# Inverse head lengths of a local-attention block: GpSimd power in place of a VectorE and ScalarE chain

## The chip, the cores and the metric

One core of a Trainium2 chip runs the whole program in one launch. The metric is device microseconds of one execution. The kernel before took 1195.36 us (median of three runs, 1194.01 to 1196.31).

## The reference

The input `x` holds 8 batches of 512 tokens by 128 features, fp32. A modulation vector made from `silu(c) @ wmod` gives each batch its shifts, scales and gates.

1. The first block ("a"): layer norm and modulation, projections to q, k, v, a 16-head attention of an unusual form (k against v, softmax, then q), gated and added to `x`. It needs 512x512 probabilities for every head and batch.
2. The second block ("b"): layer norm and modulation, then two layers (`L = 2`) of a small transformer, gated and added to `x`. Each layer does this:

```
h   = shift_token(x);  q, k, v = split(h @ wqkv)        # 8 heads of 64
q   = q / clip(norm(q), 1e-12) * qs;  k = k / clip(norm(k), 1e-12) * ksc
q, k = rotary_xpos(q, k)
o   = local_attention(q, k, v)                          # windows of 64, looking one window back
x   = x + o @ wo
h   = layernorm(shift_token(x));  x = x + (a * gelu(g)) @ w2 + b2
```

The change is about the one division `1 / clip(norm(.), 1e-12)`: for each token and head, the inverse square root of the sum of 64 squares. The scales `qs`, `ksc` are already folded into the rotary tables.

## The kernel before, in words

Block a is one stream of work called `a`: 8 batches, each 32 steps of scores on TensorE (L465), a negated row maximum on VectorE (L1191), `Exp` with row sums on ScalarE (L905), a reciprocal on VectorE (L1195), a small multiplication on GpSimd (L803) and the weighted sum on TensorE (L474).

Block b is three streams, `x`, `y`, `z` (s = 0, 1, 2), which work on the batches [0, 1, 2, 5], [3, 6] and [4, 7] in turn. Each batch passes through two layers, so there are 16 layer passes in all. Stream x starts while `a` still runs; y and z start when `a` is over. One layer pass has these parts:

- Projection of k and v, then q, one tile of 128 tokens at a time (TensorE, L523).
- Eight rotations, k's four tiles first (w = 1), then q's four (w = 0). For each: ScalarE squares the projection (L970), VectorE multiplies it by the cosine table (L1258) and, with halves swapped, by the sine table (L1262), and adds up the squares of each head (L1266, into `ss`); GpSimd adds the two products (L825, `b_rotary`). L1262 releases GpSimd's addition, L1266 comes right behind it on VectorE.
- Twice per layer pass (for k after its fourth rotation, for q after its fourth), the inverse lengths of four tiles and eight heads together, a 128x32 tile: VectorE clamps `ss` and multiplies by 2^20 (L1272, `b_norm`, which reads two SBUF tensors), ScalarE takes `Ln` (L978) and `Exp` with scale -0.5 (L980), and VectorE does a Newton step of three instructions (L1148, L1149, L1150, called from `b_rnorm`). All four VectorE instructions have two SBUF inputs. That makes 32 such chains in the program.
- GpSimd multiplies each tile by its inverse lengths (L833, `b_scale`), TensorE transposes it (L530), ScalarE copies it out (L984, L989).
- Local attention in eight units: scores (L541, L548), maximum (L1284), `Exp` in four pieces (L998), reciprocal (L1289), multiplication of the probabilities by it on GpSimd (L838), transposes (L558), weighted values (L569).
- Output projection (L579), layer norm, which has a Newton step of its own on 128x4 tiles by the same lines L1148 to L1150, hidden layer (L598), GELU (L1017), second projection (L604).

Every engine carries out its instructions strictly in the order written. That order is a string per engine (`ORDER`), which says for each next yield of work which stream it belongs to; `BANKS` says which of the eight PSUM banks each TensorE result gets. Both were laid down ahead of time. Semaphores hold each instruction until its inputs are there.

Of the kernel before, what the change touches and what calls it, by code (L numbers as in the profile page):

```python
# [65 lines left out]
B_CHAIN = LN_CHAIN + (2 * 2 + LN_CHAIN) * L  # L66
# [9 lines left out]
        "xaaaaaaaaaxxxaaxaaaaxxaaaxxaaaxxxaxxaxxxaxxxxxyxyyyyyyyxyyxxxxxxyxyyxxxxxxxxxxyyyyxxxxxxyyyyxyxxxyxx"
        "yyyxxyxxxxxyxyxxyyxxxyyxxyyyxyyxxxxxxyxxyxyyyyyyxzyzzzzzzzzzzxxxxxxzzxxzzzzxxyyyyyyyyzzzzyzxxxxxxyzz"
        "zzzzzzxxxzzxzyyzzzxzxzxxxzxyxyyxxyzxxzzxzzzzxyzxxyzxzzxzzxzzzzzyyxyxxxxxxzzxzzzzyyxxxxxyxzzxyyyzxzxx"
        "zyyyyxxzzyyxyxxxyzzzyzzzyzzzxyxxxzzzxzxzyxxxzyyyyyyzxxyzzyzxxxzxzzyzyyzxxyxxyyyyxyzxzzzxzzyyzzzzxzxx"
        "xxxxyyxyyxyyzzzzzzxxxxzxzxzzxzyzyyyxxzyxzxyzzzyyzzxxzzyzyyxzzxzxyyzyyxzyyxyzyxxyxyzxzzzyxxzzzxzxyxxy"  # L80
# [17 lines left out]
    "ACT": (
        "aaaaaaaaaaaaaaaaaaaaaaaaaaaaaaaaaaaaaaaaaaaaaaaaaaxaaaaaaxaaaaaaaaaaaaaaaaaaxaaxaaaxxxaxxxxaaxaxxaaa"
        "axxaaaxxxaaaaaxxaaaaxxxxaaaaaaaaaaaaaaaaaaaaaaaaaaaaaaaaaaaaaaaaaaaaaxxaxaxxaaaxaaaaaaaaaaaaaaaaaaxx"  # L100
        "xaxxaaxxaaxaaxaxaaaaaaxaaaaxaxaaaaxaaxaaaaxaaaxxaxxxxxxaxaxaaaaxxaaxxxaaaaxxaaaxxaxxaaaaxxaxaxxxxxax"
        "xxaxaxxaxaxaaaaxaxaxaaxaaaaaaaaaaaaxaaaxaxaaxxaxxxaxxxaaxaxaxaaaaxaaxaxxxaaxxaaaaxaxaxxaaaxxxxxxaaaa"
        "xxxxxxxxxxyyxyyxyyyyyxyyyxyyyxyxxxxxxxxxyxxyyxxxyxyxyxxyyyxxyxxyyxxxyyxxxyyxxxxxyxyxxyyxxyyyxyyxxyxy"
        "yyxzxxzzyzzzzzzzzzzxzxxxzzxxzxzzxyyxzzyyxxzzzzyyxyxzzxxxyyyzzzzxxyzzzzxxzzxzzxyyzzxxxxzxxxzxyxxyyzxx"
        "yyxzxyzxxyzzzxzzzxzzzyyxzzxzzyzxzzyyzxxxxyyxyxzzxzyzyxzxyxxyzzyxxyyyzxyxxzzyzxxzzzzzyzxzzxxxzzyxxxyz"
        "xxxxzyzxxzxyxxyyxyyxyxxzyyyyyzzzxzzzzxyyyzzzxxzzyyzyyyzzzxzzxxzzxxxzyxzyxzzxyzyyyzxxzzxzyzyyxxyyyzzz"
        "zzxzxzzyyzyzyxxxyyxxyyzxyyxxzxzyxxzyxxxxzyxxxxxzzzzzzzzyxxxzxxyzzyxzzzyzxzyyyyxyyzzyxyzzzyzxzyyyzyzx"
        "yxxzzzxyyxzxxzxyxyzyzxyxzzxyyxxxxyyyyxzzyyyyzxxxxxyzyxxyyxxxyxzxyxxxzxyxzxxyzyxxyxxxx"
    ),
    "POOL": (  # L110
        "aaaaaaaaaaaaaaaaaaaaaaaaaaaaaaaaaaaaaaxaxaxaxxxaxxaxxxaaxaaaxxaxxaaaaaaaaaaaaaaaaaaaaaaaaaxxaxaaaaaa"
        "aaaaaaxxxaxaxaaaaaaaaaaaaaaxxaaxxaxaaxxxxxxaxaaxxxxaaaaaxxxxaxxxaxaaaaaaaaaaaaaaaaxaxxaxaxaxxaxxaxax"
        "xaxxaxxaaaxaxxaxaxxxaxyyyyyyyyyyyxxxxxxxxxxxyyxyyyxxxxyyyxxxyxxxyxyxyyzzzzzzzzzzxxzzxxzzzzxxxxxxyyzx"
        "yyzxzyzxxxzxzyyzzyyyyxxxxxxyxyyyyxzzzzzzzzzzzyzyyzzxxzxzxyyxxzxyyxxxyxzzxzxxxxzzzzxxxxxxxxyyyyzzyyzz"
        "yyyyzzzzzzzzyyzzzzxyyyyxzxzxxzyyzxxyzxzxxzxzyyyxyxxyxxxxxxxxzzzzxxzzzzzyzzzyyzzyzzyyyyyyzyzyzxxzyyyx"
        "xyxzzxxxxxyyzxxyyxxxxyzyyxxyxxxxxx"
    ),
# [5 lines left out]
    "0123424024024023502350135023550224602640240240240240254024602450424602402402402402024062450140264623"  # L123
    "0340364013456022042002406234052042042042042052045204520402460240240240240240246204135024502450235024"
    "5024605240520154250235024602450246024660314603601630562402340621346260302402464016205135135602642042"
    "0642605450243503256052604010351300412140134013502350240240624601206504135123530530522301562042046230"
    "4513502466024604065060776776012023271207320170107675707675051270207007070723462146021206246036204723"
    "5072012701001701701010170170207606765606751050626743402713534036227271050512403050712705140712701315"
    "7053701256013760710362516702760717017060501273762516025676506743024067132076376023720510376341374027"
    "3062601206234175717031430214760416706570657405670650716560570176570656174707672572514750571232527660"  # L130
    "7060201707276407457123056736320156512305625407256076070176176707650214764757437015601615101637013017"
    "2370107127070360102502467310413206027607046152056135420565450135371013576560360414601763406430670471"
    "076516323521320734237401072107607076076076077"
# [1330 lines left out]
```

## Time and profile before

| what | value |
|---|---|
| median of three runs | 1195.36 us |
| the profiled execution | 1196.15 us |
| its span in the profile | 1194.3 us |
| granted TensorE clock, mean | 0.948 |
| TensorE matmul busy | 997.0 us (83%) |
| VectorE busy | 949.4 us (79%) |
| ScalarE busy | 918.2 us (77%) |
| GpSimd busy | 508.1 us (43%) |

Some 1.9 us of the profiled execution lie outside the span. A busy TensorE is not TensorE at its peak, since the ends of its matmuls are modelled. The profile's engines are PE (TensorE matmul), PEld (its weight load), DVE (VectorE), ACT (ScalarE), POOL (GpSimd), SP (SyncE). "Busy" leaves out waits. The last step of block a (L792 of batch 7) starts at 560.6 us; from there on only the streams of block b run.

### The profile page before, as it was taken

The page shows a single profiled execution, that of the slowest core. Times are in us where ns is not written, and L with a number is a line of the kernel's source. Part 1 is how long each engine was busy: PE and PEld are TensorE (multiplying, and loading weights), DVE is VectorE, ACT ScalarE, POOL GpSimd, SP SyncE. Part 2 cuts the span into 40 slices and gives each one's busy share as a digit, 9 for nine tenths or more (in the row PEclk, how much of TensorE's full clock was granted, in tenths as well). Part 3 has the DMA queues.
Part 4 walks back from the last instruction along what each step waited for, and adds up shares of the span by engine and source line. Part 5 has one row for each costly group of instructions (what it writes and reads, how often), then busy time and mean ns, then how long its engine had stood idle before and what let it go on. Part 6 is the DMA issues. An engine that isn't in the chain of part 4 may idle for free. (4 is left out here: it accounts for less than half of the span.)

```text
span 1194.3 us, 23996 instructions
## 1 busy us (share of the span) xinstructions
PE 997.0 (83%) x8124; PEld 510.0 (43%) x8124; DVE 949.4 (79%) x1947; ACT 918.2 (77%) x2782; POOL 508.1 (43%) x578
## 2 busy tenths in 40 slices
PE   2677787768888798778868897899999789999898
PEld 2232232223323352234336444655664357545664
DVE  4789898888869777986884699779769976789865
ACT  1698979899978988887659566868886587958983
POOL 5012143212105321343474058647823676348830
PEclk8699989999989898998989998999999999999999
DMA  5541305232204103001011001101110020001200
GB/s 206 180 142 36 106 1 146 62 107 71 72 0 130 43 28 115 10 10 24 1 31 34 10 1 32 33 1 32 33 41 10 10 63 16 18 1 32 46 20 27
DMA packets 28009, 59.18 MB, mean 50 GB/s; under 512 B 6192, under 2 KB 6384, under 8 KB 26736
## 3 DMA queue, kind: packets, MB, share of 16 engines
q1 hardware_dynamic: 27120, 56.33, 16.7%
q8 instruction: 67, 1.10, 0.4%
q10 hardware_dynamic: 768, 1.31, 0.3%
q14 instruction: 54, 0.44, 0.1%
HBM read 23.98 MB, written 18.87 MB: 36 GB/s over the span
## 5 line engine op out<-in xcount | busy, mean ns | idle before, releaser
L905 ACT ACTIVATE E<-psum,neg_max 128x512 f32<-128x512 f32 x512 | 346.6, 716 | 64.2 <-DVE neg_max L1191 45.9
L1191 DVE TENSOR_REDUCE neg_max<-psum 128x2 f32<-128x1024 f32 x256 | 307.5, 1214 | 58.7 <-PE psum L465 56.7
L465 PE MATMUL psum<-v_rows,k_rows 64*128 64x512 f32 x512 | 130.3, 514 | 106.0 <-ACT E L905 79.6
L998 ACT ACTIVATE rot_work<-psum,neg 128x128 f32<-128x128 f32 x512 | 184.3, 412 | 17.9 <-DVE neg L1284 11.0
L838 POOL TENSOR_TENSOR rot_work<-rot_work,rz 128x512 f32<-128x512 f32 x128 | 133.0, 1047 | 141.0 <-DVE rz L1289 140.9
L825 POOL TENSOR_TENSOR work<-work,rot_work 128x512 f32<-128x512 f32 x96 | 121.7, 1273 | 129.6 <-DVE rot_work L1262 129.3
L465 PEld LDWEIGHTS psum<-v_rows,k_rows 64*128 64x128 f32 x512 | 52.8, 196 | 250.6 <-ACT E L905 116.1
L803 POOL TENSOR_TENSOR qz<-qT,rz 128x32 f32<-128x32 f32 x128 | 30.8, 241 | 300.7 <-DVE rz L1195 299.8
L523 PE MATMUL psum<-wqkv_sb,hs 128*128 128x512 f32 x288 | 144.0, 622 | 6.8 <-DVE hs L1248 3.8
L474 PE MATMUL psum<-E,qz 128*32 128x512 f32 x1024 | 148.2, 653 | 0.2 <-POOL qz L803 0.2
L998 ACT ACTIVATION_READ_ACCUMULATOR rot_work<-psum,neg 128x1 f32 x512 | 126.7, 252 | 0.0
L905 ACT ACTIVATION_READ_ACCUMULATOR E<-psum,neg_max 128x1 f32 x512 | 119.8, 234 | 0.0
L1284 DVE TENSOR_REDUCE neg<-psum 128x4 f32<-128x512 f32 x128 | 85.5, 677 | 36.2 <-PE psum L548 36.1
L833 POOL TENSOR_TENSOR work<-work,rn 128x512 f32<-128x512 f32 x96 | 99.6, 1056 | 16.6 <-DVE rn L1150 16.6
L970 ACT ACTIVATE rot_work<-psum 128x512 f32<-128x512 f32 x128 | 77.9, 612 | 31.0 <-PE psum L523 22.3
L598 PE MATMUL psum<-work,w_sb 128*128 128x512 f32 (+1 forms) x192 | 94.0, 623 | 2.7 <-ACT work L1013 2.1
L558 PE MATMUL psum<-ident,rot_work 128*128 128x128 f32 x512 | 80.8, 286 | 15.5 <-POOL rot_work L838 8.8
L1008 ACT ACTIVATE prT<-psum 128x512 f32<-128x512 f32 x128 | 79.2, 636 | 11.5 <-PE psum L569 8.2
L1262 DVE TENSOR_TENSOR rot_work<-psum,rot 128x512 f32<-128x512 f32 x128 | 87.0, 679 | 0.0
L1266 DVE TENSOR_REDUCE ss<-rot_work 128x8 f32<-128x512 f32 x128 | 86.4, 675 | 0.0
L558 PEld LDWEIGHTS psum<-ident,rot_work 128*128 128x128 f32 x512 | 57.1, 143 | 45.6 <-POOL rot_work L838 26.3
L1258 DVE TENSOR_TENSOR work<-psum,rot 128x512 f32<-128x512 f32 x96 | 65.4, 681 | 12.6 <-ACT rot_work L970 12.3
(140 smaller groups left out, 1784.7 us busy)
## 6 DMA issues: line engine op xcount, KB each, us to landing
k_rows<-k_scr SPq DMA_DIRECT2D x128, 64.0 KB, 1.9
work<-v_al SPq DMA_DIRECT2D x16, 512.0 KB, 4.4
v_rows<-v_scr SPq DMA_DIRECT2D x124, 64.0 KB, 1.9
...
```

The source lines that it names most:

```text
L465: pe.matmul(bank, k_rows[r:r + 64, half, hh, P * j:P * (j + 1)], v_rows[r:r + 64, b % 2, hh, :], start=True, stop=True).then_inc(full, 1)
L474: last = pe.matmul(O_BANK[32 * q:32 * q + 32, :], qz[:, hh, j % QZ_SLOTS, q, :], E[:, (b * NG + g) % E_RING, q, :], start=(g == 0), stop=( ...
L523: pe.matmul(bank, hs[s][:, P * i:P * (i + 1)], wqkv_sb[:, l, INNER * c:INNER * (c + 1)], start=True, stop=True).then_inc(full, 1)
L558: last = pe.transpose(bank[:, P * w:P * (w + 1)], pr[s][:, u % PR_SLOTS, w, :], ident[:])
L598: pe.matmul(bank[0:CH[c]], w1_sb[:, l, o:o + CH[c]], h2T[s], start=True, stop=True).then_inc(full, 1)
L825: pool.tensor_tensor(qk_of(s, i, w), qk_of(s, i, w), sinp[s][:, n % 2, :], ALU.add).then_inc(rot_sum[s], 1)
L833: pool.tensor_tensor(v, v, rn[s][:, i, w, :].unsqueeze(2).broadcast_to([P, H, DH]), ALU.mult).then_inc((q_ready, k_ready)[w][s], 1)
L838: pool.tensor_tensor(pr[s][:, u % PR_SLOTS], pr[s][:, u % PR_SLOTS], rz2[s][:, u, :].unsqueeze(2).broadcast_to([P, 4, 2 * W]), ALU.mult).t ...
L905: act.activation(E[:, (b * NG + g) % E_RING, 2 * half + m, :], pair[:, m], ACT.Exp, bias=neg_max[:, n, m:m + 1], accum_out=z[:, n, m:m + 1 ...
L998: last = act.activation(pr[s][:, u % PR_SLOTS, w, :], bank[:, 2 * W * w:2 * W * (w + 1)], ACT.Exp, bias=neg2[s][:, u, w:w + 1], accum_out= ...
L1191: dve.tensor_reduce(neg_max[:, n, :], pair, AX.X, ALU.max, negate=True).then_inc(max_ready, 1)
L1262: dve.tensor_tensor(sinp[s][:, n % 2, :].rearrange("p (h a r) -> p h a r", h=H, a=2), bank.rearrange("p (h a r) -> p h a r", h=H, a=2)[:, ...
```

## The change

The chain of six instructions becomes two on GpSimd: a clamp and multiplication by 2^20 (`tensor_scalar`, one SBUF input, into `nt`), and `nt` to the power of a tile that holds -0.5 (`tensor_tensor` with `ALU.pow`, into `rn`). There is no Newton step. GpSimd waits for the sums (`ss_ready`) itself, then waits for its own first instruction. The tile `clamp` (2^20 everywhere, set up by a GpSimd memset at L781) becomes `minus_half`; `nlog` and two sets of semaphores go. The chain on VectorE and the two activations go from their streams, and GpSimd's stream gets them: for k after its fourth rotation, for q after its eighth. `ORDER` and `BANKS` are new on all engines; every other instruction stays as it is.

```diff
-B_CHAIN = LN_CHAIN + (2 * 2 + LN_CHAIN) * L
+B_CHAIN = LN_CHAIN + LN_CHAIN * L
 ORDER = {
...
-            pool.memset(clamp[:], SHIFT2).then_inc(s_clamp, 1)
+            pool.memset(minus_half[:], -0.5).then_inc(s_minus_half, 1)
...
+            def b_norm(s, k, l, w):            # pool
+                n = (k * L + l) * 2 + 2 - w
+                passed(pool, ss_ready[s], (k * L + l) * 2 * J + J * (2 - w))
+                pool.tensor_scalar(nt[s][:, :, w, :], ss[s][:, :, w, :], NORM_MIN2, SHIFT2, ALU.max, ALU.mult).then_inc(ss_all[s], 1)
+                pool.wait_ge(ss_all[s], n)
+                pool.tensor_tensor(rn[s][:, :, w, :], nt[s][:, :, w, :], minus_half[:], ALU.pow).then_inc(rn_ready[s], 1)
...
+                            if n == J - 1:
+                                b_norm(s, k, l, 1)
+                                yield
                             for i in {J: (0,), J + 1: range(1, J)}.get(n, ()):
                                 b_scale(s, k, l, i, 1)
                                 yield
+                        b_norm(s, k, l, 0)
+                        yield
                         for i in range(J):
                             b_scale(s, k, l, i, 0)
                             yield
...
-            def b_norm(s, k, l, w):            # act
-                act.wait_ge(ss_all[s], (k * L + l) * 2 + 2 - w)
-                act.activation(nlog[s][:, :, w, :], ss[s][:, :, w, :], ACT.Ln).then_inc(ss_log[s], 1)
-                act.wait_ge(ss_log[s], (k * L + l) * 2 + 2 - w)
-                act.activation(rn[s][:, :, w, :], nlog[s][:, :, w, :], ACT.Exp, scale=-0.5).then_inc(ss_rsqrt[s], 1)
...
-            def b_norm(s, k, l, w):            # dve
-                passed(dve, ss_ready[s], (k * L + l) * 2 * J + J * (2 - w))
-                v = ss[s][:, :, w, :]
-                dve.scalar_tensor_tensor(v, v, NORM_MIN2, clamp[:], ALU.max, ALU.mult).then_inc(ss_all[s], 1)
-
-            def b_rnorm(s, k, l, w):
-                dve.wait_ge(ss_rsqrt[s], (k * L + l) * 2 + 2 - w)
-                newton(ss[s][:, :, w, :], rn[s][:, :, w, :], nt[s][:, :, w, :], b_link_of(s, k)).then_inc(rn_ready[s], 1)
```

## Rows read from the trace of the kernel before

**Rows 1.** The page: busy us (share of the span) and instructions of each engine.
```profile
PE 997.0 (83%) x8124; PEld 510.0 (43%) x8124; DVE 949.4 (79%) x1947; ACT 918.2 (77%) x2782; POOL 508.1 (43%) x578
```
**Rows 2.** Busy time by stretch: us, each engine's busy (instructions), clock, DMA share.
```profile
0.00:562.00 562.00, 429.34 (x2861) 176.01 (x2862) 453.13 (x802) 461.93 (x1375) 163.05 (x266) 0.91 0.27 79
562.00:1194.00 632.00, 567.66 (x5271) 334.01 (x5266) 496.30 (x1146) 456.27 (x1407) 345.02 (x313) 0.98 0.10 23
```
**Rows 3.** The same view, PE PEld DVE ACT POOL, of eleven 20 us stretches.
```profile
600.00:620.00 20.00, 11.40 (x52) 6.50 (x51) 18.21 (x31) 9.43 (x22) 16.78 (x16) 0.89 0.00 0
...
700.00:720.00 20.00, 19.79 (x58) 8.60 (x58) 19.83 (x37) 12.67 (x26) 15.52 (x14) 1.00 0.00 1
...
940.00:960.00 20.00, 12.33 (x45) 6.47 (x46) 19.23 (x45) 8.43 (x17) 13.33 (x12) 0.75 0.04 14
...
1100.00:1120.00 20.00, 18.07 (x236) 12.11 (x234) 19.37 (x38) 17.32 (x67) 18.82 (x18) 1.00 0.21 48
sum 220.00, PE 196.18 PEld 99.97 DVE 211.75 ACT 151.34 POOL 156.15; mean PE 17.83 PEld 9.09 DVE 19.25 ACT 13.76 POOL 14.20
```
**Rows 4.** VectorE and ScalarE by line, from 562 us: xcount, busy us, mean ns, idle before.
```profile
L1272 DVE SCALAR_TENSOR_TENSOR ss<-ss,clamp 128x32 f32<-128x32 f32 x26 | 17.2, 666 | 0.3
L1149 DVE TENSOR_TENSOR nt<-nt,rn 128x32 f32<-128x32 f32 x26 | 14.1, 543 | 0.9
L1148 DVE SCALAR_TENSOR_TENSOR nt<-ss,rn 128x32 f32<-128x32 f32 x26 | 12.3, 472 | 2.9 <-ACT rn L980 2.8
L1150 DVE SCALAR_TENSOR_TENSOR rn<-nt,rn 128x32 f32<-128x32 f32 x26 | 7.3, 281 | 0.9
L978 ACT ACTIVATE nlog<-ss 128x32 f32<-128x32 f32 x26 | 6.6, 253 | 4.8 <-DVE ss L1272 4.5
L980 ACT ACTIVATE rn<-nlog 128x32 f32<-128x32 f32 x26 | 6.0, 229 | 0.8
```
**Rows 5.** Line L1272 alone, VectorE: busy (xcount) in the eleven stretches, their sum.
```profile
600.00:620.00 20.00, 1.85 (x3) 0.89 0.00 0
...
sum 220.00, DVE 12.08; mean DVE 1.10
```
**Rows 6.** In order of time, one chain near 1096 us, with VectorE, GpSimd and ScalarE.
```profile
1095.93 1.27 DVE L1272 SCALAR_TENSOR_TENSOR ss<-ss,clamp 128x32 f32<-128x32 f32 x1
...
1098.32 0.67 DVE L1266 TENSOR_REDUCE ss<-rot_work 128x8 f32<-128x512 f32 x1
...
1099.83 1.01 DVE L1149 TENSOR_TENSOR nt<-nt,rn 128x32 f32<-128x32 f32 x1
1100.87 0.19 DVE L1150 SCALAR_TENSOR_TENSOR rn<-nt,rn 128x32 f32<-128x32 f32 x1
```
**Rows 7.** GpSimd in order of time, the same stretch.
```profile
1095.88 1.28 POOL L825 TENSOR_TENSOR work<-work,rot_work 128x512 f32<-128x512 f32 x1
1098.48 1.27 POOL L825 TENSOR_TENSOR work<-work,rot_work 128x512 f32<-128x512 f32 x1 [1.32 <-DVE rot_work L1262]
1099.75 1.04 POOL L838 TENSOR_TENSOR rot_work<-rot_work,rz 128x512 f32<-128x512 f32 x1
```
**Rows 8.** The whole program by line: GpSimd's instructions nearest to the two added.
```profile
L803 POOL TENSOR_TENSOR qz<-qT,rz 128x32 f32<-128x32 f32 x128 | 30.8, 241 | 300.7 <-DVE rz L1195 299.8 <-PE psum L474 0.9
L838 POOL TENSOR_TENSOR rot_work<-rot_work,rz 128x512 f32<-128x512 f32 x128 | 133.0, 1047 | 141.0 <-DVE rz L1289 140.9
L782 POOL MEMSET k_rows<- 128x4096 f32 x1 | 3.5, 3505 | 0.0
```
**Rows 9.** Waits from 562 us: us in total, times, the longest in us.
```profile
POOL work L833 <- DVE rn L1150: 13.2, 11, 4.9
POOL prT L833 <- DVE rn L1150: 5.3, 12, 0.6
...
PE psum L530 <- POOL work L833: 5.8, 5, 3.0
PE psum L530 <- POOL prT L833: 5.7, 3, 3.2
```

More of the change, by code:

```diff
@@ L76 @@
[L76 to L80, printed above, removed]
@@ new lines @@
+        "aaaaxxaaxxxaxaaaaxaaaxxxaaaxxxaaaxaaxaaaaaaaaaaxaaaaaaxxxxaaxxxxaaaaxaaaaaaaxaaxxxxxxaaaxxxxaaaaaaxx"
+        "xxxxaaaaaaxaaxxxaaaaxaaxxaaaxaaxaxxaxxxxxxyxxxyxyyxyyyyyyyxxxxxxxyyxyyyxxxxxxxxxxyyyxxxxxxyyyyxxxxyx"
+        "xyyyxxxxxyxyxxxyyxyxyxxxyxyyxyyxxxxxxxyxyxyyyyyyzxzzzzzzzzzzxxxxxzzxzzzzxxxxyzzzyzyzzyyxxxxxzyxzyzzz"
+        "yyyzzyzzzxxxzzxzxxzzxxxzxyxyyxxyzyxxxzzzzxzzyzxxyzxzzxyyzxzzyzzzzxyxxxxxxzzzxzzzyxxxyxyyzzzxxzxxyyxz"
+        "xyzyyyzzyzxxzyyxyxyzyzzyzzxzxxxxxzyzzyxzxyyyyyxyxxyxxzxxyxxxzyyyyxyxxyzxyyyxzzxzzzzyzxyyzxyxxxxxyxzy"
@@ L83 @@
+        "yxzzzzzzzzzzyyyyyyzzxzzzzxxxyxxxxxzzzxzxzzyyyyzzzxxyzzzxxxxzzzyyzyzzxzxzxzyyxyzyxxyyxzxxzzxzyzzzxzxx"
+        "yzzzzzxxxzzzzzyyyxxxyyzzxzzzxyzyzzzxyyyyyyyxyyyxzxzxzxyxxyxzzzyyzxzxxyyzzzyyzyyxxxxzxxxyzzzyxxzxxzxx"
+        "yyyyyxyyxxzyyxyxyxyyzxyxxxyxxxzyxzxzxzyzzxyyxxyxyxyyxyzxyzxxxxxxxx"
     ),
@@ L95 @@
-        "yxyyxxzyyxzzxzzyzzyzxyxzzyxzxzxxzzyzxxyyzzyzyyyxxyxyyxzyyzyyyxyyxxyzxxxxyzzxyxxxxxzyxzxyyxxxyxyzzzxx"
-        "xxyyxyxzyzyxxxxx"
+        "aaaaaaaaaaaaaaaaaxaaxxxaaaxaxaaaaaaaaaaxaaaxaaaaaaaaaaaaxaaaaaaaaaaaaaaaaaaaaaaaaaaaaaaaaaaaaaaaaaaa"
+        "aaaaaaaaaaaaaaaaaaaaaaxxaxxxxaaaaaaxaaaaaaaaaaaaaaaaaaaaaaaaaaaaaaaaaaaaaaxxaaxxxxxaxxxaaaxaaaxaaaaa"
+        "aaxaaaaxaaaaxaxaaaxaaaaaaxxaaaxaaaxaaaaaaaxaaaxxaaxaaaxaaaxaaaxaaaaaxxaaaaaaaaaaxaaaaxxaxaxxxaaaxaax"
+        "xxxaaxaaaaxaxaaxxxaaxaxaaaxaxaaaaaaaaaxaxaaxaaaaaaaxxxxaaaaaaxxaxaaaxaaaaxxaxaaxaxxaaaaxaxaaaaaaaxaa"
@@ new lines @@
+        "aaaxxaxxxxaaaxaaxxaxxaxxxyxxxyxxyxyxxxyxyyyyxxxyxxyxxxxxxxxyyyyyxyyxyxyxxyxxxxxxxyyyxxxxxxyyyxyxyxyx"
+        "xyxyxyyxxxyyxxxzyyzxzyxzzzzzzxxzzxxyyxzxzzyzzyzzzxxzzzzyzzzyzzzyzzxyxxzxxxxxzzxzxxxzxxxyxxxyxzzzzzxz"
+        "xzxxxzxzzzyxyxxyyzxxzyyyxyxyyzxxyyzzxyzzyyzzxyyzyzyzyxyxzzzyyzzyzzzyzxzxxzxxxxyyyxyxyyxxxyzxxzxyxxzx"
+        "xyzxyyxyyxxxzzzxyzzzyxxxzyxzxxzzzzzxzyyyzxyyzyyxyxxxzzzxzzzzyyxzyyzzyxzzzxzzzzyzyzyyzyzyzzxyzxxzyxxx"
+        "xyxyxxyzzzxyzxzxxxzzzxxzxxzzxyyzxzxxyyyxyxyyyzyzzyxxzzxzzyzxxzzyzzzxxzzzzyzxzxxxyyzyyzyyyxxzzyyyyyyy"
@@ L97 @@
+        "zyyyxxxyzxxyxxxyxxyyxxxxyxyxxxzzzxxxyxxyyxxyzyzxxxxx"
     ),
     "ACT": (
[L99 to L102, printed above, removed]
@@ L108 @@
-        "yxxzzzxyyxzxxzxyxyzyzxyxzzxyyxxxxyyyyxzzyyyyzxxxxxyzyxxyyxxxyxzxyxxxzxyxzxxyzyxxyxxxx"
+        "aaaaaaaaaaaaaaaaaaaaaaaaaaaaaaaaaaaaaaaaaaaaaaaaaaxaaaaaaxaaaaaaaaaaaaaaaaaaxaaaaaaxxxxxxaxxxxaaaaxa"
+        "aaaaaxxxaxxaaaaaaaaaxxxxaaaaaaaaaaaaaaaaaaaaaaaaaaaaaaaaaaaaaaaaaaaxxaxaxxaaaxaaaaaaaaaaaaaaaaaaaaaa"
+        "aaaxaxxxxaxxaaxaaxxaaaaaaxaaaaaxaaaxaaxaaaaxaaaaaxaxaxxxxxaxxaaxaaaxaxaaxxxaaxaaxxaaaxxaaaaxxaxaaaxx"
+        "xaxxxaxaaxaxaxxaxaxaaaxaaaaaaaxaxaaxaaaaaaxaxaxaxaxxxaxxaxxxaxaxaxxaxxxaaaaaaxxxxaaaxxaxaaxxaxxxxxxx"
@@ new lines @@
+        "yxxyxxyyxyyyxyyyyxyyxyyyxyyxxxxxxxxxxyyyxxxxxxyyyxxyxxyyyxxxxxxyyxxxxyyxxyxxyyxxyyxyyxxyxyyyzxzzxxzz"
+        "zzzzzzzzxxxxzxzxzzzzxxxxzyzzyzyyzzzxxzzxzxxxyyyzzzzyyzyzyxzzxxzxzxxxxzxxxzxyxxyyxzxyyxzxyzxxyzzzyxyz"
+        "zzxyzzzxzxyzzyzzxzzxyxxyyyxzzzyxzxxxyxyyzzxyyzzyxyzzxyxyzxzzyzzzyxxzzxxyxxzzxxyxxxxxxyxxzyxyxxyzyyyx"
+        "yxxyzyyyxzxyxyyyxzyzyzyzzzxzzzzzzyyzyyzzxyzzxzzyxxyxxyxxyzxxzzzxxzzyzyzzzzxxyzyxxzzyxzzzzxyzyzxxyxyz"
+        "xyyzxxxxzxxxyzyxzxxyzzzxzzxzzzxzzxyxxzzzzzxzzyzzyxyyyyyxyyyzyxzyzyzzzxyzyzxzxxyyzzyyzyyzxxzxxzxxxzzy"
@@ L109 @@
+        "yyxxxxxxyyyyyxzyyyxyxxyyzxxyyxxxxzxyxxxxyzyxxxxxyxxxx"
     ),
     "POOL": (
[L111 to L114, printed above, removed]
@@ L115 @@
-        "yyyyzzzzzzzzyyzzzzxyyyyxzxzxxzyyzxxyzxzxxzxzyyyxyxxyxxxxxxxxzzzzxxzzzzzyzzzyyzzyzzyyyyyyzyzyzxxzyyyx"
-        "xyxzzxxxxxyyzxxyyxxxxyzyyxxyxxxxxx"
+        "aaaaaaaaaaaaaaaaaaaaaaaaaaaaaaaaaaaaaaaxaxxxxaxxxxaxxaaaxaxxaxaaxxaxaaaaaaaaaaaaaaaaaaaaaaaaxxaaxaaa"
+        "aaaaaaaaaaaxaxxxaxaaaaaaaaaaaaaaaaxxaxaxxaxxaxxxxaxxxaxaxxxaaaxaxaxaxaxaaxaxxaaaaaaaaaaaaaaxxxaxxxxx"
+        "xaxxxaxxxaxxaxaaxxaxaxaaxxxxyyyyyyyyyyyyyyxyxxyxxxxxxxxyxyxxxxxxyyyxyxxxyxxxyxyyzzzzzzzzzzzxzzzxzzzz"
+        "xxxxxxxxzxzzxyyxzxyzzxxxzxzyyyyyxxyxyyxxxyxyxyyyyyzzzzzzzzzzzyzzzyzzzzxxyyxxxxyzzyxxzyxyzxxxxxzxxzxx"
@@ L117 @@
+        "zzxxxxxxxxyyyyyyyyyyyyyyyyyyzzzzzzzzzzzzyzzyzzzzxxxyxxxzzxxyzzxxxxzyxzxzxzxxxyyyxxxxxxzzzzxxzzzzzzzz"
+        "zzzzzzyyyyyyyyyyzzyyzzyyzyyyyxxzzxzxxxxxxyxyyxxxxxyxxyxyyyxxxxxxxx"
     ),
     "SP": (
-        "aaaaaaaaaaaaaaaaaaaaaaaaaaaaaxaaaaaaaaaaaaaaaaaaaaaaaaaaaaaaaxaaaaaaaaaxaxyxxzxyzxyzxzyxzyxzyx"
+        "aaaaaaaaaaaaaaaaaaaaaaaaaaaaaaxaaaaaaaaaaaaaaaaaaaaaaaaaaaaaaxaaaaaaaaaaxxyxxzxyzxyzxyzxzyxyzx"
     ),
@@ L122 @@
 BANKS = (
[L123 to L133, printed above, removed]
+    "0123424024024023502350135023550224602640240240240240254024602450424602402402402402024026450124604205"
+    "0346026402362406453015302530153502402402402402540254025402460240240240240240246204135024502450235024"
+    "5024024024602306430246135013502320254025305320250642542054502402450102630652450202460240123420462660"
+    "4125024502540136015302530253402345042013502402350322560256203520350244601260310565302466010220426054"
+    "2052042604204366076076017010760105070661547654765676567606567040706705060546572406122352026352075623"
+    "6527656076776076076767607607767076707670161710126501060715717524067123047415104364502560353403160230"
+    "7206417214630217430651460670170607607601560671750760730107127104214031231043240236351035106054375767"
+    "6072650265234701721462317634654356076570265164712375646706547547654756760576570670767570767540502654"
+    "6450740164270213201357207451745617064306747062634767476575460432702710425671401476034710373137241032"
+    "0470121701701706712726054075615370571031507401371540532423402340213025650132103602107207654207260725"
+    "672376560752460374054253101340120120120120120"
 )
@@ L176, in build @@
         x_sb = sb("x_sb", [P, B, J, D])
-        clamp = sb("clamp", [P, J, H])
+        minus_half = sb("minus_half", [P, J, H])
         gate_col = sb("gate_col", [D, 2, 2 * B])
@@ L198, in stream_tensors @@
             r["v_al"] = one("v_al", [P, J, INNER])
-            for n in ("ss", "rn", "nt", "nlog"):
+            for n in ("ss", "rn", "nt"):
                 r[n] = one(n, [P, J, 2, H])
@@ L248, in build @@
         up = [[v[:, n, :] for n in range(3)] for v in v_al]
-        ss, rn, nt, nlog = (each(n) for n in ("ss", "rn", "nt", "nlog"))
+        ss, rn, nt = (each(n) for n in ("ss", "rn", "nt"))
         kT, qT2 = each("kT"), each("qT2_")
@@ L273, in build @@
         s_silexp, s_sil, s_setup = sem("s_silexp"), sem("s_sil"), sem("s_setup")
-        s_gcol, s_tables, s_clamp, s_qz, s_kzero = (
-            sem(n) for n in ("s_gcol", "s_tables", "s_clamp", "s_qz", "s_kzero"))
+        s_gcol, s_tables, s_minus_half, s_qz, s_kzero = (
+            sem(n) for n in ("s_gcol", "s_tables", "s_minus_half", "s_qz", "s_kzero"))
         s_chain = sem("s_chain")
```

41 lines of the change are left out of this document (4 added, 37 removed).

## The prediction

> **What bounds the kernel now.** I read the page's busy shares first: TensorE 83%, VectorE 79%, ScalarE 77%, GpSimd 43% [rows 1]. No engine is full, so the average says little, and I cut the span at 562 us, where block a ends [rows 2]. Up to there ScalarE is the busiest (461.93 of 562 us), with VectorE right behind (453.13). After it TensorE has 567.66 of 632 us, VectorE 496.30, GpSimd 345.02. The reader is to see that these are means over unlike stretches. Cut into pieces of 20 us, block b has eleven pieces in which VectorE is busy for at least 18.2 of 20 us; together they are 220 us with VectorE at 211.75, that is 96% [rows 3]. They are where two streams rotate at once. TensorE issues few matmuls there (52 in 600 to 620 us, 45 in 940 to 960), has 11.40 and 12.33 us busy, and its granted clock falls to 0.89 and 0.75 as a mean of a stretch in which it does little. So block b alternates between stretches that VectorE sets and stretches that TensorE sets. The chains that the change touches are dense in the former: 18 of block b's 26 clamps lie in the eleven pieces (the counts of the view of line L1272 alone add up to 18; its row with three is shown) [rows 4, 5].
>
> **What is removed.** In block b the four VectorE instructions of a chain take 17.2 + 14.1 + 12.3 + 7.3 = 50.9 us over 26 chains, 1.96 us each [rows 4]. Block a has the other six of the 32 chains, at the same mean at most 6 x 1.96 = 11.8 us. ScalarE loses 6.6 + 6.0 = 12.6 us in block b [rows 4] and in block a six times the same 0.253 + 0.229 = 0.482 us, 2.9 us.
>
> Most of the 1.96 us is not work. An L1272 that starts at 1095.93, just after a GpSimd addition started at 1095.88 for 1.28 us, takes 1.27 us; an L1149 at 1099.83 takes 1.01 us and ends with the GpSimd multiplication of 1099.75 to 1100.79, while the L1150 behind it, with GpSimd idle, takes 0.19 us [rows 6, 7]. These instructions stand still until GpSimd's has ended, and VectorE, which goes in order, stands with them. No instruction with two SBUF inputs on VectorE is left in the new chain, so the stalls go with it; the four instructions at an undisturbed 0.19 us each would be 0.76 of the 1.96.
>
> **What is added.** Per chain two GpSimd instructions on a 128x32 tile. The first, with one input, I take at 0.2 us, just under the 0.241 us of a two-input multiplication of the same shape [rows 8]. The power is in no row. Its lower end is that multiplication, 0.24 us. Its upper end I take from the longest simple instruction of GpSimd, 3.5 us [rows 8]; nothing in the trace excludes even more. Between these I take 1.05 us, the row of a 128x512 multiplication: it does sixteen multiplications for each of the power's elements, which is a plausible amount of work for one power. So a chain costs GpSimd 1.25 us, and block b 26 x 1.25 = 32.5 us on top of 345.02.
>
> The Trainium skill speaks against moving such work: "GPSIMD Engine Reference", section "Engine selection", gives elementwise work to VectorE and calls GpSimd about twice as slow for two inputs. The rows agree in direction for the same shape (0.241 against 0.19 us). As a price for the power, twice VectorE's 0.19 us would be 0.4 us, an estimate by that page; GpSimd would then get 0.6 us a chain and the gain would be safer, not of another sign.
>
> **Does the added wait cost?** The GpSimd clamp waits for the fourth L1266. That one starts at 1098.32 and ends at 1098.99; the addition L825 that stands before the new clamp runs from 1098.48 to 1099.75 [rows 6, 7]. So the sums are there 0.76 us before GpSimd gets to them, and the wait costs nothing. If the merge put the clamp elsewhere it would be at most the 0.67 us of L1266. The wait of the power for the clamp is on one engine, counted in the 0.2 us. Queued behind the power on GpSimd are the same stream's scalings (which need it anyway), the next rotation additions, and other streams' multiplications of probabilities, for which TensorE's transposes wait.
>
> The latency gets shorter: the chain of 1095.93 has its result at 1101.06, 5.1 us later [rows 6]; the new one needs 1.3 to 1.4 us. GpSimd no longer idles for the Newton step (13.2 + 5.3 = 18.5 us in block b), and TensorE's waits on the scaled tiles, 5.8 + 5.7 = 11.5 us, can shrink [rows 9]. With the stall gone, what is late next in a rotation is GpSimd's own addition and scaling.
>
> **The sum.** It is made against the profiled execution of 1196.15 us, which is 0.79 us above the median.
> - Block a: ScalarE is its bound, six chains on it are worth 2.9 us, which I take. The ends are 0 (the maxima and `Exp` wait for each other in turns) and VectorE's 11.8.
> - The dense pieces of block b: 18 x 1.96 = 35.3 us of VectorE time go. That would be the gain if VectorE alone set the pace. But GpSimd is at 156.15 of the 220 us [rows 3], and gets 18 x 1.25 = 22.5: 178.7 us, which in 220 - 35.3 = 184.7 us would be 97%. Its best piece is 18.82 of 20, 94% [rows 3], so GpSimd stops the gain at 220 - 178.7/0.94 = 30 us, and two in-order engines that feed each other don't both run full. I take a third of 35.3, 11.8 us. The ends are 0 and 30.
> - The other 8 chains of block b lie where TensorE sets the pace: 0, at most 8/26 of the 11.5 us that it waits for scaled tiles, 3.5 us.
> - The new order and banks: by itself neither gain nor loss that I can price; every order of instructions shifts some waits, and of TensorE's 64 us without work in block b (632 less 567.66) any part could move. I keep 4 us either way.
>
> 1196.15 - 2.9 - 11.8 = 1181.45 us for a profiled execution, 1180.7 for a median: I forecast 1181.
>
> **Rivals.**
> 1. The freed time turns to idle time: VectorE waits for TensorE instead, and only block a gains. For it speaks that TensorE shows 196.18 of 220 us busy even in the dense pieces [rows 3]; against it, that so few matmuls stand behind that figure. Time: 1195.4 - 2.9 = 1192.5.
> 2. GpSimd becomes the bound of the rotations and gives the gain back. In 1100 to 1120 us it is at 18.82 of 20 already [rows 3]. Were it the bound throughout, the 22.5 us that it gets in the dense pieces would be added, less the 18.5 us that it waited for the Newton step: +4, less 2.9 in block a: 1196.5. Against it: its mean there is 71%.
> 3. Slower: the power is expensive. Place: the in-order GpSimd queue of the dense pieces. With c the price of one power, GpSimd needs there 156.15 + 18 x (0.2 + c), and at 94% fills 220 us from c = 2.6 us on. At c = 3.5 us it needs 222.8/0.94 = 237 us: 17 us longer, and six powers in block a hold up the small multiplication on which its ring depends, so I credit nothing there. Time: 1212; each further us of c adds 18/0.94 = 19 us. For it speaks that no row shows GpSimd doing more than one simple operation per element; against it, that 16 multiplications' worth of time is only 1.05 us. The Trainium skill makes this rival worse: by "SBUF — State Buffer", section "Who interferes with whom", a VectorE instruction with two SBUF inputs and a GpSimd instruction that reads SBUF exclude each other, and the later waits for the whole of the other. The trace agrees to within 0.05 us [rows 6, 7]. By it a long power would also hold up VectorE at the layer norms' Newton steps, which remain of that kind, by up to 3.5 us each time that they meet.
> 4. The change doesn't do what it says, that is, the stall of L1272 and L1149 passes to the layer norms' L1148 and to copies of `hs`, which meet a busier GpSimd. With 26/2 = 13 layer passes in block b and one stall of 1.04 us [rows 7] in each it is 13.5 us at most, partly in stretches that TensorE sets; half of it takes the forecast to 1188, and I count it in its upper half.
>
> **How the numbers follow.** Forecast 0.55, its own range 1166 to 1191 (below, 1195.4 - 2.9 with 27 of the dense pieces' possible 30 us gained; above, 4 us gained in all). Rival 1: 0.15. Rival 2: 0.12. Rival 3: 0.18. What a measurement of this kernel can tell from no change is about 0.2%, 2.4 us. Faster: 0.55, 0.08 of rival 1 (2.9 us is on the edge) and 0.03 of rival 2, 0.66. Within it: 0.07 + 0.06 = 0.13. Slower: 0.18 + 0.03 = 0.21. For 8 in 10 the range reaches from 1166 over rivals 1 and 2 to 1204, which leaves out most of rival 3 and little below.
>
> **What would show it.** Right: VectorE's busy time falls by 51 us and more and ScalarE's by 15; the dense pieces of block b get shorter with VectorE under 95% and GpSimd at 80% or more; the power's row has about 1 us; GpSimd's wait for L1150 is gone and nothing of its size takes its place before the scalings. Rival 1: the same falls, but longer idle times of VectorE behind TensorE. Rival 2: GpSimd at 90% in many pieces, and transposes L530 and L558 that wait for it. Wrong altogether: a power of 2.6 us or more, or a time of block a that moves by more than 6 us either way, since only six chains lie there and the order would then be the cause.

## The result and the profile after

The changed kernel takes 1330.77 us (median of four runs, 1329.82 to 1331.88) against 1195.57 us for the kernel before in the same runs: a ratio of 1.1133, 95% interval 1.1114 to 1.1152. The forecast was 1181 us, the range ended at 1204. It is 135 us slower, and the prediction is wrong.

The page of the kernel after, its busy line, the granted clock per slice, and two rows of its groups (busy us, mean ns | idle before):

```profile
PE 1044.7 (79%) x8124; PEld 542.1 (41%) x8124; DVE 900.5 (68%) x1819; ACT 907.3 (68%) x2718; POOL 688.7 (52%) x642
...
PEclk8799889989986899798789888998999798898899
...
L832 POOL TENSOR_TENSOR rn<-nt,minus_half 128x32 f32<-128x32 f32 x32 | 174.4, 5449 | 2.7
...
L1262 DVE TENSOR_TENSOR rot_work<-psum,rot 128x512 f32<-128x512 f32 x128 | 87.2, 681 | 21.1 <-POOL work L824 21.1
```

One row stands out: a power of 128x32 takes 5.449 us, the same to within 11 ns in all 32 (the line's own view has 5447 to 5458 ns). The chain's removal shows too, somewhat smaller than the signs in the prediction had it (51 us and more, and 15): against [rows 1], VectorE lost 48.9 us of busy time and ScalarE 10.9. GpSimd gained 180.6, of which 174.4 are powers.

The busy time of two stretches, cut where block a ends (its last addition starts at 582.8 us now, at 560.6 before):

```profile
0.00:584.00 584.00, 434.07 (x2804) 176.12 (x2804) 446.42 (x772) 455.61 (x1345) 193.39 (x274) 0.89 0.26 76
584.00:1328.00 744.00, 610.64 (x5320) 366.01 (x5320) 454.08 (x1048) 451.73 (x1374) 495.27 (x369) 0.91 0.08 20
```

Beside [rows 2]: block a is 22 us longer with six powers, block b 112 us longer with 26. GpSimd is busy for 67% of block b, TensorE for 82% and the others for less. By these averages nothing is full. The views of 20 us (PE, PEld, DVE, ACT, POOL, clock) show where:

```profile
640.00:660.00 20.00, 8.55 (x36) 5.42 (x36) 9.37 (x16) 6.54 (x12) 19.83 (x16) 0.66 0.00 0
...
1020.00:1040.00 20.00, 12.87 (x104) 7.52 (x102) 14.43 (x34) 7.57 (x15) 19.63 (x13) 0.89 0.24 58
...
1060.00:1080.00 20.00, 14.44 (x208) 10.43 (x207) 11.59 (x23) 12.50 (x51) 19.83 (x15) 0.84 0.21 48
```

In 640 to 660 us GpSimd has no gap, VectorE is busy for 9.37 of 20 us where such a stretch had 18 to 20 before [rows 3], and TensorE, with 8.55 us busy, has a mean granted clock of 0.66, between its two levels of 1.2 and 2.4 GHz. The same stretch in order of time, all engines (start us, us, engine, line):

```profile
643.62 1.12 PE L529 MATMUL psum<-ident,prT 128*128 128x128 f32 x4 [0.78 <-POOL prT L839]
...
644.78 0.60 ACT L989 ACTIVATE qT<-psum 128x512 f32<-128x512 f32 x1 [0.45 <-PE psum L529]
644.89 0.32 POOL L830 TENSOR_SCALAR nt<-ss 128x32 f32<-128x32 f32 x1
644.96 0.68 DVE L1262 TENSOR_TENSOR rot_work<-psum,rot 128x512 f32<-128x512 f32 x1
645.29 5.45 POOL L832 TENSOR_TENSOR rn<-nt,minus_half 128x32 f32<-128x32 f32 x1
645.56 0.68 DVE L1266 TENSOR_REDUCE ss<-rot_work 128x8 f32<-128x512 f32 x1
650.71 1.26 POOL L824 TENSOR_TENSOR prT<-prT,rot_work 128x512 f32<-128x512 f32 x1
651.93 1.04 POOL L839 TENSOR_TENSOR work<-work,rn 128x512 f32<-128x512 f32 x1
...
653.02 1.12 PE L529 MATMUL psum<-ident,work 128*128 128x128 f32 x4 [8.28 <-POOL work L839]
...
653.93 1.92 PE L522 MATMUL psum<-wqkv_sb,hs 128*128 128x512 f32 x2
...
655.88 0.60 ACT L981 ACTIVATE rot_work<-psum 128x512 f32<-128x512 f32 x1 [1.11 <-PE psum L522]
...
656.51 0.69 DVE L1258 TENSOR_TENSOR work<-psum,rot 128x512 f32<-128x512 f32 x1 [10.28 <-ACT rot_work L981]
```

From 646.24 to 650.71 us no other engine works. The last rows show the way by which the power holds the others up. A scaling (L839) waits for the power; TensorE's transpose (L529) waits 8.28 us for that scaling; the projection of another rotation (L522) stands behind the transpose in TensorE's queue; ScalarE squares that projection (L981), and only then VectorE goes on, after 10.28 us. There is a second way: the additions of the next rotations also stand behind the power, and VectorE's L1262 may run at most two rotations ahead of them, since `sinp` has two slots. It is the smaller one here. Before, VectorE waited 12.3 us in all for the squares at this place, and its waits list none for a slot; now it is 74.0 and 21.1 us. The waits that hang on GpSimd, longest in total first (us in total, times, longest), of the kernel after:

```profile
DVE work L1258 <- ACT rot_work L981: 74.0, 33, 10.3
...
PEld psum L529 <- POOL work L839: 71.0, 28, 8.7
PE psum L529 <- POOL work L839: 53.6, 14, 8.3
...
PE psum L557 <- POOL rot_work L844: 39.6, 18, 4.6
...
PE psum L529 <- POOL prT L839: 23.4, 10, 4.6
DVE rot_work L1262 <- POOL work L824: 21.1, 6, 6.4
```

In block b alone, TensorE's matmuls waited 5.8 + 5.7 us for scaled tiles before [rows 9], and 6.5 us for multiplied probabilities; from 584 us on it is now 43.6 + 18.8 us and 38.3 us.

### The profile page after: what moved, and what is told of

It reads as the page before. It is cut to its first block, busy times and chain, and to the rows that moved or that the text cites. A ratio compares the mean times of both kernels' runs of the same rounds, so it can differ in the third digit from the quotient of the medians.

```text
span 1328.0 us, 23866 instructions
## 1 busy us (share of the span) xinstructions
PE 1044.7 (79%) x8124; PEld 542.1 (41%) x8124; DVE 900.5 (68%) x1819; ACT 907.3 (68%) x2718; POOL 688.7 (52%) x642
## 4 chain that ended last, share of the span: by engine, by line
PE 36%; DVE 22%; POOL 22%; ACT 9%; issue 9%; DMA 1%; SPq 1%; ACTq 0%; DVEq 0%; POOLq 0%
DVE neg_max L1191 9%; POOL rn L832 9%; PE psum L597 4%; PE psum L522 4%; POOL work L824 4%; ACT E L916 4%; PE psum L473 4%; PE psum L568 3%; PE psum L464 3%; PE psum L578 3%; PE psum L557 3%; POOL rot_work L844 3%; PE psum L529 2%; POOL work L839 2%; PE psum L603 2%
## 5 line engine op out<-in xcount | busy, mean ns | idle before, releaser
L464 PE MATMUL psum<-v_rows,k_rows 64*128 64x512 f32 x512 | 133.7, 526 | 103.5 <-ACT E L916 75.5
L832 POOL TENSOR_TENSOR rn<-nt,minus_half 128x32 f32<-128x32 f32 x32 | 174.4, 5449 | 2.7
L473 PE MATMUL psum<-E,qz 128*32 128x512 f32 x1024 | 151.8, 668 | 7.0 <-POOL qz L802 7.0
L522 PE MATMUL psum<-wqkv_sb,hs 128*128 128x512 f32 x288 | 150.3, 648 | 2.1 <-ACT kT L994 0.7
L981 ACT ACTIVATE rot_work<-psum 128x512 f32<-128x512 f32 x128 | 77.3, 605 | 62.4 <-PE psum L522 38.0
L557 PE MATMUL psum<-ident,rot_work 128*128 128x128 f32 x512 | 85.3, 297 | 40.4 <-POOL rot_work L844 39.6
L529 PE MATMUL psum<-ident,work 128*128 128x128 f32 x384 | 71.5, 328 | 56.8 <-POOL work L839 53.6
L1262 DVE TENSOR_TENSOR rot_work<-psum,rot 128x512 f32<-128x512 f32 x128 | 87.2, 681 | 21.1 <-POOL work L824 21.1
L839 POOL TENSOR_TENSOR work<-work,rn 128x512 f32<-128x512 f32 x96 | 99.2, 1049 | 0.0
```

Source lines behind the costliest of these rows:

```text
L464: pe.matmul(bank, k_rows[r:r + 64, half, hh, P * j:P * (j + 1)], v_rows[r:r + 64, b % 2, hh, :], start=True, stop=True).then_inc(full, 1)
L473: last = pe.matmul(O_BANK[32 * q:32 * q + 32, :], qz[:, hh, j % QZ_SLOTS, q, :], E[:, (b * NG + g) % E_RING, q, :], start=(g == 0), stop=( ...
L522: pe.matmul(bank, hs[s][:, P * i:P * (i + 1)], wqkv_sb[:, l, INNER * c:INNER * (c + 1)], start=True, stop=True).then_inc(full, 1)
L557: last = pe.transpose(bank[:, P * w:P * (w + 1)], pr[s][:, u % PR_SLOTS, w, :], ident[:])
L832: pool.tensor_tensor(rn[s][:, :, w, :], nt[s][:, :, w, :], minus_half[:], ALU.pow).then_inc(rn_ready[s], 1)
```

## The experiments

Each run is compared with the kernel before on the same chip. Where a table gives us, it is the ratio times 1195.36.

### What a power costs

`prices`, executed once, has the minimum of `dose0` (below), and behind the last work of GpSimd

```diff
+                price(pool.tensor_tensor(r[:, 0:1, 0, :], v[:, 0:1, 0, :], half[:, 0:1, :], ALU.pow))
+                price(pool.tensor_tensor(r[:, 0:2, 0, :], v[:, 0:2, 0, :], half[:, 0:2, :], ALU.pow))
+                price(pool.tensor_tensor(r[:, :, 0, :], v[:, :, 0, :], half[:], ALU.pow))
+                price(pool.tensor_tensor(r[0:32, :, 0, :], v[0:32, :, 0, :], half[0:32], ALU.pow))
+                price(pool.tensor_tensor(r[:, :, 0, :], v[:, :, 0, :], half[:], ALU.mult))
```

> The changed kernel with every power replaced by a one-input minimum against 7.1e-5 (so the inverse lengths are a constant of the right size and the output is not the reference's), and behind the last work of GpSimd a list of instructions measured one by one: powers of 8, 16 and 32 elements per partition on 128 partitions, one of 32 elements on 32 partitions, and a multiplication of 32. Theory 1, a power costs per element: about 0.1 us + 0.167 us per element, so 1.4, 2.8 and 5.45 us, and the same 5.45 us on 32 partitions, since each of the eight processors works through its own 16. Theory 2, a fixed cost (a library call, a table): about 5.4 us whatever the size. The multiplication 0.24 us.

The five in order of time:

```profile
1138.96 1.67 POOL L897 TENSOR_TENSOR rn<-nt,minus_half 128x8 f32<-128x8 f32 x1
1140.71 2.90 POOL L898 TENSOR_TENSOR rn<-nt,minus_half 128x16 f32<-128x16 f32 x1
1143.69 5.42 POOL L899 TENSOR_TENSOR rn<-nt,minus_half 128x32 f32<-128x32 f32 x1
1149.19 5.42 POOL L900 TENSOR_TENSOR rn<-nt,minus_half 32x32 f32<-32x32 f32 x1
1154.68 0.25 POOL L901 TENSOR_TENSOR rn<-nt,minus_half 128x32 f32<-128x32 f32 x1
```

From 8 to 32 elements it is 3.75 us, 0.156 us per element and 0.4 us fixed; a quarter of the partitions saves nothing. Theory 1 holds, with a larger fixed part than its 0.1 us. A two-input multiplication goes by (1047 - 241)/480 = 1.7 ns per element [rows 8], so a power is some 90 multiplications per element, not 16.

### How the time follows GpSimd's added time

`dose0`, `dose1` and `dose2` keep the new order and all of the change but compute 0, 1 and 2 of the four tiles by the power, and a minimum against a constant does the rest. The edit of `dose2`:

```diff
-                pool.tensor_tensor(rn[s][:, :, w, :], nt[s][:, :, w, :], minus_half[:], ALU.pow).then_inc(rn_ready[s], 1)
+                pool.tensor_tensor(rn[s][:, 0:2, w, :], nt[s][:, 0:2, w, :], minus_half[:, 0:2, :], ALU.pow)
+                pool.tensor_scalar(rn[s][:, 2:J, w, :], nt[s][:, 2:J, w, :], 7.1e-5, None, ALU.min).then_inc(rn_ready[s], 1)
```

> The changed kernel, its order and its clamp, but the power replaced by a one-input minimum against 7.1e-5 (a constant, output not the reference's), so c is about 0.3 instead of 5.45 us. Theory 1, the power's time in GpSimd's queue is the whole loss and the relief of VectorE is real: faster than before, 1175 to 1188 us (the forecast's mechanism). Theory 2, the new order is itself bad, or the relief is worth nothing: 1193 us or more.

> As dose0, but two of the four tiles of each power are computed (128x16) and the minimum does the other two: c about 2.75 + 0.3 = 3.05 us. If the loss grows in proportion to GpSimd's added time: half way between dose0 and the changed kernel, about 1255 us. If it starts only from a threshold near c = 2.6 us, as the prediction had it: 1195 to 1205 us, and then 19 us or more for each us.

> As dose0, but one of the four tiles of each power is computed (128x8, 1.65 us as measured alone) and the minimum does the other three: a chain costs GpSimd some 2.3 us, against 0.63 us in dose0 and 3.5 us in dose2. Straight between the two runs (25.5 us for each us): 1172 + 1.65 x 25.5 = 1214 us. With a threshold as the prediction had it (nothing below 2.6 us of power): under 1185 us.

The added instructions of `dose0`, and of `dose2`:

```profile
L830 POOL TENSOR_SCALAR nt<-ss 128x32 f32<-128x32 f32 x32 | 10.7, 334 | 2.7
...
L832 POOL TENSOR_SCALAR rn<-nt 128x32 f32<-128x32 f32 x32 | 9.4, 292 | 2.6
```
```profile
L832 POOL TENSOR_TENSOR rn<-nt,minus_half 128x16 f32<-128x16 f32 x32 | 93.7, 2929 | 2.7
...
L830 POOL TENSOR_SCALAR nt<-ss 128x32 f32<-128x32 f32 x32 | 10.6, 332 | 2.7
...
L833 POOL TENSOR_SCALAR rn<-nt 128x16 f32<-128x16 f32 x32 | 8.4, 262 | 2.2
```

| kernel | GpSimd us per chain | ratio, 95% interval | us | each further us per chain costs |
|---|---|---|---|---|
| dose0 | 0.63 | 0.9796 (0.9754 to 0.9838) | 1171.0 | |
| dose1 | 2.28 | 1.0102 (1.0072 to 1.0133) | 1207.6 | 22 us |
| dose2 | 3.52 | 1.0414 (1.0379 to 1.0449) | 1244.8 | 30 us |
| changed | 5.77 | 1.1133 (1.1114 to 1.1152) | 1330.8 | 38 us |

An added us per chain is 32 us of GpSimd in the program, so 0.69, 0.94 and 1.19 of it land in the time. By the intervals the three slopes are good to about 4, 4 and 2 us: the bend from the first to the last is clear of noise, a single step of it is not. A threshold of the prediction's size is refuted, since dose1 and dose2 lie 23 and 40 us above what it allowed; they come in 6 and 10 us under the straight line, and dose0 4 us under its range. With 22 us for each us, dose0's 24.4 us of gain are used up at 0.63 + 1.1 = 1.7 us a chain, that is, at a power of 1.4 us; this is an estimate between two runs. dose1, with a power of 1.67 us, is 1% slower than the kernel before. The last step costs more than GpSimd's own time. TensorE's waits are part of it, and so may be its clock: the mean granted clock is 0.951 in dose0, 0.942, 0.937, and 0.900 in the changed kernel, and TensorE's busy time for the same 8124 matmuls goes from 1009.7 us in dose2 to 1044.7. How the step divides between them was not measured apart.

### The order

`pow_old_order` and `cheap_old_order` are the changed kernel and dose0 with `ORDER` and `BANKS` of before, the chain's letters moved from VectorE's and ScalarE's strings to GpSimd's.

> The changed kernel's instructions in the order and with the banks of the kernel before: the chain's yields taken out of VectorE's and ScalarE's orders, GpSimd's put behind the fourth rotation and right before the scaling of q. Theory 1, the price of the power is the cause: about as slow as the changed kernel, 1310 to 1350 us. Theory 2, the new order carries a good part of the loss: under 1290 us.

> dose0's instructions (GpSimd clamp, a minimum in place of the power, output not the reference's) in the order and banks of the kernel before. With the power the new order was 29 us faster than the old one. If an order's worth is that it makes room for GpSimd's two instructions, it is small where they are short: 1172 to 1185 us here, against 1172 in the new order. If the old order is generally worse for the changed set of instructions: 1195 us or more.

The first has 1.1355 (1.1312 to 1.1399), that is 1357 us, somewhat above the range of its theory 1, so the new order is worth 0.0222 x 1195 = 27 us with the full power. The second has 0.9969 (0.9957 to 0.9981) against dose0's 0.9796: 21 us. Both expectations for it were missed: 1191.6 us lies between them. The order is not to blame for the loss; it is the larger part of dose0's gain. In the old order even the cheap chain on GpSimd gained only 4 us.

### Occupation of the queue or wait of the consumers

`power_late` is dose0 with a full power behind the last scaling, its result unused. `power_split` is the changed kernel with four powers of 8 elements, each before its tile's scaling.

```diff
+                if i == J - 1:
+                    pool.tensor_tensor(nt[s][:, :, w, :], nt[s][:, :, w, :], minus_half[:], ALU.pow).then_inc(p_chain, 1)
```
```diff
-                pool.tensor_tensor(rn[s][:, :, w, :], nt[s][:, :, w, :], minus_half[:], ALU.pow).then_inc(rn_ready[s], 1)
...
+                pool.tensor_tensor(rn[s][:, i, w, :], nt[s][:, i, w, :], minus_half[:, i, :], ALU.pow).then_inc(rn_ready[s], 1)
```

> dose0 with a full power of 5.45 us per chain, but behind the last scaling of its four tiles, its result unused (output not the reference's). GpSimd is occupied exactly as in the changed kernel, and the chain to this stream's own scalings, transposes and scores is short. If occupation of the in-order queue is the loss: 1320 to 1360 us, as the changed kernel. If the wait of the power's own consumers is the loss: under 1250 us. In between, the shares can be read off.

> The changed kernel with each power cut into four of 8 elements, each right before the scaling of its tile. 4 x 1.65 = 6.6 us of GpSimd instead of 5.45, but no block is longer than 1.7 us and the first scaled tile comes 3.8 us sooner. If occupation counts: 1.15 us more a chain at 38 us for each, 1375 us. If the length of one block counts: under 1320 us.

`power_late` has 1.087 (1.0809 to 1.093), 1299 us: of the 160 us between dose0 and the changed kernel, 128 come back although nobody needs the result. So 80% comes from occupying the queue alone. The other 20% may be the wait of the power's own consumers, or that the power stands at another place of the queue; the run doesn't tell these apart. In its waits the multiplied probabilities have taken the place of the scaled tiles:

```profile
PE psum L558 <- POOL rot_work L851: 65.4, 26, 5.7
DVE rot_work L1269 <- POOL work L825: 37.5, 10, 8.5
...
PE psum L530 <- POOL work L842: 13.6, 8, 4.7
PE psum L530 <- POOL prT L842: 12.4, 10, 3.7
```

`power_split` has 1.1168 (1.113 to 1.1206), level with the changed kernel, with 210.9 us of powers instead of 174.4. Neither expectation came in: 36 us more on GpSimd cost about 4 us, which is within the noise. So the shorter blocks, or the first tile that comes earlier, take off about as much as the longer occupation adds.

### What VectorE's relief is worth by itself

`act_only` keeps the order of before and leaves of the chain ScalarE's two activations. It drops the Newton step, so its inverse lengths are only as exact as the tables of `Ln` and `Exp`, and it adds 1e-24 x 2^20 where before clamps.

```diff
-            pool.memset(clamp[:], SHIFT2).then_inc(s_clamp, 1)
+            pool.memset(clamp[:], NORM_MIN2 * SHIFT2).then_inc(s_clamp, 1)
...
-                act.wait_ge(ss_all[s], (k * L + l) * 2 + 2 - w)
-                act.activation(nlog[s][:, :, w, :], ss[s][:, :, w, :], ACT.Ln).then_inc(ss_log[s], 1)
+                passed(act, ss_ready[s], (k * L + l) * 2 * J + J * (2 - w))
+                act.activation(nlog[s][:, :, w, :], ss[s][:, :, w, :], ACT.Ln, scale=SHIFT2,
+                               bias=clamp[:, 0, 0:1]).then_inc(ss_log[s], 1)
...
-                act.activation(rn[s][:, :, w, :], nlog[s][:, :, w, :], ACT.Exp, scale=-0.5).then_inc(ss_rsqrt[s], 1)
+                act.activation(rn[s][:, :, w, :], nlog[s][:, :, w, :], ACT.Exp, scale=-0.5).then_inc(rn_ready[s], 1)
```

> The kernel before in its own order, with only ScalarE's two activations left of the chain: Ln reads the sums with scale 2^20 and a bias of 1e-24 x 2^20 in place of the clamp, Exp writes the inverse lengths, there is no Newton step (so they are as exact as the two tables). VectorE loses all 57 us, GpSimd gets nothing. Theory 1, VectorE's time and stalls in the chain cost real time: 1168 to 1182 us. Theory 2, dose0's gain came from the new order or from ScalarE: 1188 us or more.

`newton_pool` keeps both activations and puts the clamp and the whole Newton step on GpSimd:

```diff
+                p_link(pool.tensor_tensor(t, v, r, ALU.mult))
+                p_link(pool.tensor_tensor(t, t, r, ALU.mult))
+                p_link(pool.tensor_scalar(t, t, -0.5, 1.5, ALU.mult, ALU.add))
+                pool.tensor_tensor(r, t, r, ALU.mult).then_inc(rn_ready[s], 1)
```

> The kernel before in its own order, with ScalarE's Ln and Exp kept, and the clamp and the Newton step (as four instructions) on GpSimd: some 0.33 + 3 x 0.25 + 0.3 us and the waits between them, 1.7 us a chain, and no VectorE. Theory 1, VectorE's relief is worth what dose0 showed (24 us) and each us on GpSimd costs 25: 1172 + 1.1 x 25 = 1199 us, no gain. Theory 2, only a long single block on GpSimd hurts, short ones slip in: 1175 to 1188 us.

`clamp_one_input` changes one instruction of the kernel before:

```diff
-                dve.scalar_tensor_tensor(v, v, NORM_MIN2, clamp[:], ALU.max, ALU.mult).then_inc(ss_all[s], 1)
+                dve.tensor_scalar(v, v, NORM_MIN2, SHIFT2, ALU.max, ALU.mult).then_inc(ss_all[s], 1)
```

> The kernel before in its own order, with the clamp on VectorE as an instruction of one SBUF input (max, then times 2^20) instead of two. If the stall comes from the second SBUF input: the clamp's row falls from 607 to about 170 ns, 14 us of VectorE go, 1186 to 1193 us. If a one-input instruction stalls as well, or the stall only moves to the next instruction: 1195 to 1199 us.

`act_only`: 0.988 (0.9853 to 0.9907), 1181 us. Theory 1 holds: 50 us less VectorE (899.1 busy) and nothing on GpSimd give 14 us in the old order. Nearly all of it comes in block b: block a's last addition starts at 560.1 us, against 560.6 before. It is faster than both kernels. `newton_pool`: 1.0144 (1.012 to 1.0168), 1213 us, 32 us above `act_only` for five short instructions that add up to 1.29 us a chain: 25 us for each us, near the first step of the doses. But GpSimd also stands in its queue until ScalarE's `Exp` is there, 13.6 us in all or 0.43 us a chain; with this it is 18 us for each us. Theory 2, that only long blocks hurt, falls. Theory 1's 1199 us is missed by 14 us, since it took VectorE's relief at dose0's 24 us, and `act_only` shows 14 in this order. `clamp_one_input`: 0.9998 (0.998 to 1.0016), no change, and the line's own view shows why (ns, least, median, most):

```profile
L1272 DVE TENSOR_SCALAR ss<-ss x32: 149/738/1269, 159.1 to 1122.6; 128x32 f32<-128x32 f32 x32
```

The one-input form stalls up to 1269 ns like the two-input form, 595 ns in the mean against 607.

### Both together

`act_only_new_order` is `act_only` in the new order; ScalarE's pairs stand where the trace of dose0 had GpSimd's minimum.

> act_only's instructions (Ln with scale and bias, Exp, no Newton step, nothing of the chain on VectorE or GpSimd) in the new order and banks; GpSimd's norm yields are taken out, and each pair of activations stands in ScalarE's order where the trace of dose0 had GpSimd's minimum. The order was worth 19 us with cheap GpSimd instructions (1191.35 against 1172.0), and act_only's 1179.7 was 11.7 us under the former. If both effects add: 1157 to 1166 us. If the new order only makes room for GpSimd's work, which is not there now: 1174 to 1182 us.

It has 0.9907 (0.9889 to 0.9926), 1184 us: 2 us above the range of the second theory, and 3 us above `act_only` in the old order, which the overlapping intervals don't tell from nothing. The effects don't add. The new order gained 21 us and 27 us where GpSimd had the chain, and nothing where ScalarE had it. No version that computes the inverse lengths is faster than `act_only`.

## Why the prediction was wrong

- **What bounds the kernel now, what is removed.** Right in the main. Relief of VectorE is real: `act_only` takes 50 us off it and gains 14.3 us, nearly all in block b. That the forecast's terms, 2.9 + 11.8 = 14.7 us, add up to nearly the same is luck: the 2.9 us stood for ScalarE's two activations in block a, which `act_only` keeps and no run isolates, and the 11.8 was a third of 35.3 us with a loaded GpSimd beside it. The stall was laid to VectorE's second SBUF input; `clamp_one_input` shows that an instruction with one stalls as well. This changes nothing in the sum, as the new chain has no instruction on VectorE.
- **What is added: the price of the power.** This is the step that failed first. I took 1.05 us because sixteen multiplications per element seemed enough, and took 3.5 us, a row of a memset, as the upper end, though I wrote that nothing excluded more. Measured: 5.449 us. The first instruction was 0.32 us instead of 0.2.
- **Does the added wait cost?** Right for the sums: the 32 clamps on GpSimd have 2.7 us of idle time before them in all, 0.08 us each. Wrong for the latency, which was to fall from 5.1 to 1.3 or 1.4 us: the new chain takes 5.8 us [rows 6].
- **The sum, GpSimd's limit.** This failed too, and would have even with the right price. The prediction let GpSimd take time for nothing until it filled the dense pieces at 94%, from c = 2.6 us on, and charged 19 us for each us beyond. By that rule 5.45 us give 1212 + 1.95 x 19 = 1249 us; the kernel takes 1331. The doses show 22 us for each us of a chain in the first step, rising to 38, and a break-even at a power of about 1.4 us. With my own 1.05 us the chain would be 1.38 us and, on the doses' first slope, an estimated 1171 + 0.75 x 22 = 1188 us: a gain inside the stated range, but half of the forecast's. The rows around 645 us show why: in every rotation GpSimd stands between VectorE and TensorE, and TensorE's queue holds the next projections behind the transpose that waits for it. So GpSimd's share of a 20 us piece says little about how long the others can do without it.
- **The new order.** I kept 4 us either way; it was worth 21 us at dose0 and 27 us with the power, and nothing clear of noise for `act_only`.
- **Rivals.** 3 named the place and the sign, with chance 0.18, a bound that was too low, and no cost in block a, which is 22 us longer than before and 26 us longer than in dose0, whose order it shares (its last addition starts at 556.8 us). 1 would leave block b without a gain, and `act_only` gains there. 2's time, a gain just given back, is what the doses give for a GpSimd chain of 1.7 us. 4 hardly showed: the layer norms' own L1148 (128x4, 24 times) takes 342 ns in the mean after and 375 before, L1150 (128x4, 32 times) 233 after and 162 before, 2 us in all.
- **The Trainium skill's rule in rival 3** was that a long GpSimd instruction with SBUF inputs would lock out VectorE's two-input ones. This case's measurement differs, as the next section but one shows, and the measurement decides.
